# A recurrent two-layer kernel: the experts' gates travel through a DRAM scratch instead of a selection product

## The reference, cut to what matters

```python
xn = layernorm(x)
scores = sigmoid(xn @ gate_w.T)                  # 32 experts
choice = scores + gate_bias                      # 4 groups of 8; best 2 groups, then best 8 experts
w = scores[chosen]; w = w / (w.sum(-1) + 1e-20) * 2.5
g = einsum('th,eih->eti', xn, expert_gate); u = einsum('th,eih->eti', xn, expert_up)
outs = einsum('eti,ehi->eth', silu(g) * u, expert_down)
final = (outs[chosen] * w).sum(1) + shared_mlp(xn)
x = x + attention(xn) * silu(final)
```

## Time and profile before

| what | value |
|---|---|
| median of 3 runs | 594.4 us (592.83 to 595.43) |
| the profiled execution | 595.31 us |
| its span, first to last instruction | 593.6 us |
| outside the span | 1.7 us |
| mean granted clock of PE | 0.953 |
| loop of the first layer's pairs | 44.8 to 243 us of the span |
| scan and second layer | about 250 to 593.6 us |

### The profile page before, as it was taken

How to read it: one execution, slowest core, us unless ns; L and a number is a source line. 1 busy time by engine, 2 the same in 40 slices (tenths; PEclk the granted TensorE clock), 3 DMA queues, 4 the chain that set the end, 5 groups by cost and what they waited for, 6 DMA issues and landing times.

```text
span 593.6 us, 8790 instructions
## 1 busy us (share of the span) xinstructions
PE 532.1 (90%) x2918; PEld 411.9 (69%) x2918; DVE 476.1 (80%) x857; ACT 291.4 (49%) x791; POOL 378.4 (64%) x326
## 2 busy tenths in 40 slices
PE   3978999999999999595899999999999999999865
PEld 3745656666566666384788888888888888888634
DVE  7667775885786586359988999999999999999885
ACT  4431242243225224313666766676667667766523
POOL 6930010012203254443899999999999999999963
PEclk9988999999999999859799999999999999999777
DMA  8440000000000000010011121111111120011002
GB/s 240 154 142 0 2 1 1 1 1 7 12 0 2 18 1 0 15 40 0 19 37 39 33 55 37 31 42 36 54 32 42 36 55 23 31 37 36 19 1 71
DMA packets 16601, 20.81 MB, mean 35 GB/s; under 512 B 2344, under 2 KB 10160, under 8 KB 16428
## 3 DMA queue, kind: packets, MB, share of 16 engines
q1 hardware_dynamic: 16556, 20.26, 11.5%
HBM read 9.76 MB, written 1.05 MB: 18 GB/s over the span
## 4 chain that ended last, share of the span: by engine, by line
POOL 42%; PE 34%; DVE 13%; issue 9%; ACT 1%; DMA 0%; POOLq 0%; DVEq 0%; ACTq 0%
PE bank L560 32%; POOL shared L502 14%; POOL shared L510 7%; POOL shared L488 7%; POOL shared L494 7%; POOL shared L517 6%; PE bank L563 2%; DVE shared L1459 1%; DVE shared L1293 1%; DVE shared L1298 1%; DVE bank L1434 1%; POOL state_ext L524 1%; DVE shared L1216 1%; DVE shared L1208 1%; DVE shared L1428 1%
## 5 line engine op out<-in xcount | busy, mean ns | idle before, releaser
L560 PE MATMUL bank<-xnT_lo,wgu_hi 128*128 128x512 f32 x264 | 121.7, 461 | 11.1 <-ACT shared L1096 7.8
L560 PE MATMUL bank<-w,shared 128*128 128x128 f32 x1024 | 123.6, 279 | 0.3
L560 PEld LDWEIGHTS bank<-w,shared 128*128 128x128 f32 x1024 | 117.7, 193 | 6.2 <-ACT shared L1096 6.2
L560 PE MATMUL bank<-xnT_hi,wgu_lo 128*128 128x512 f32 x264 | 106.0, 402 | 0.0
L560 PE MATMUL bank<-xnT_hi,wgu_hi 128*128 128x512 f32 x264 | 104.9, 397 | 0.0
L502 POOL TENSOR_TENSOR shared<-shared 128x1024 f32<-128x1024 f32 x36 | 86.3, 2399 | 24.6 <-DVE shared L1459 24.6
L560 PE MATMUL bank<-shared 128*128 128x512 f32 (+3 forms) x280 | 90.5, 444 | 2.0 <-ACT shared L944 1.2
L966 ACT ACTIVATE shared<-bank 128x512 f32<-128x512 f32 x68 | 40.6, 597 | 99.0 <-PE bank L560 93.3
L1459 DVE TENSOR_TENSOR shared<-shared,bank 128x2048 f32<-128x2048 f32 x36 | 82.0, 2278 | 5.7 <-PE bank L560 5.7
L1434 DVE TENSOR_REDUCE bank<-shared 128x64 f32<-128x2048 f32 x36 | 82.4, 2288 | 0.3
L1096 ACT ACTIVATE shared<-bank,b 128x512 f32<-128x512 f32 x128 | 81.7, 699 | 0.0
(11 more groups left out here) (175 smaller groups left out, 805.6 us busy)
## 6 DMA issues: line engine op xcount, KB each, us to landing
w<-in_w SPq DMA_DIRECT2D x8, 256.0 KB, 3.1
shared<-in_w SPq DMA_DIRECT2D x1, 2048.0 KB, 9.4
left_tok<-state_ext SPq DMA_DIRECT2D x16, 128.0 KB
left_tok<-state_ext SPq DMA_DIRECT2D x8, 192.0 KB
shared<-in_wd SPq DMA_DIRECT2D x1, 1088.0 KB, 11.8
x<-in_x SPq DMA_DIRECT2D x4, 256.0 KB, 3.5
out<-x SPq DMA_DIRECT2D x4, 256.0 KB, 2.3
left_tok<-state_ext SPq DMA_DIRECT2D x4, 254.0 KB
```

The lines of the kernel that those rows point to most:

```text
L560: return nc.tensor.matmul(out, lhsT, rhs, start=start, stop=stop)
```

## The change

`gate_rows` on PE, its matrix `pair_row`, bank `GB`'s use in the loop, and the split of the gates into three parts are gone. ACT now writes the 32 x 512 gates of a batch in float32 to `gate0T`. SP stores them in a DRAM scratch, waits for the store, and then loads each pair's two rows of 512 gates, each spread over 64 partitions, into a ring of three tiles `gate_rows`. A load for pair n is issued once `h0` of pair n - 3 is made. DVE multiplies by the tile in SBUF and waits for its two DMAs. SP's queue runs in order, so the first two shifts of the scan stand between the loads of later pairs now: `shift(0)` behind those of pair 36, `shift(1)` behind those of pair 52.

```diff
@@ SP
+            def rows_of_gates(n):
+                b, p = divmod(n, PAIRS)
+                if p == 0:
+                    sp.wait_ge(s("g0T_cp"), b + 1)
+                    sp.dma_start(gates_d[b], gate0T[:, b % 2]).then_inc(s("st_gates"), 16)
+                    sp.wait_ge(s("st_gates"), 16 * (b + 1))
+
+                after(sp, s("h0_done"), n - RING + 1)
+                for m in range(2):
+                    sp.dma_start(gate_rows[m * I0:(m + 1) * I0, n % RING],
+                                 gates_d[b, 2 * p + m].partition_broadcast(I0)).then_inc(s(f"ld_rows{n % RING}"), 16)
...
             sp.wait_ge(s("ld_identity"), 16 * B)
+            for n in range(B * PAIRS):
+                rows_of_gates(n)
+                if n == 2 * PAIRS + 4:
+                    shift(0)
+                elif n == 3 * PAIRS + 4:
+                    shift(1)
             for k in range(LEVELS * B):
-                shift(k)
+                if k > 1:
+                    shift(k)
@@ POOL
-            g.tensor_copy(ident_bf[:], ident[:]).then_inc(cdone, 1)
...
-            g.tensor_copy(pair_row[:], pair_sel[:].unsqueeze(2).broadcast_to([3 * E0, E0, I0])).then_inc(sel, 1)
@@ PE
-            def gate_rows(n):
-                b, p = divmod(n, PAIRS)
-                if p == 0:
-                    pe.wait_ge(s("g0T_cp"), b + 1)
-                after(pe, s("h0_done"), n)
-                sel = pair_row[:, 2 * p:2 * p + 2].rearrange("p e i -> p (e i)")
-                mm(bank[GB][:], sel, gate0T[:, b * N:(b + 1) * N]).then_inc(s("gb_mm"), 1)
...
-                    last = tr(bank[MISC if b == 0 else AT][:].bitcast(BF16)[0:3 * E0, j * P:(j + 1) * P],
-                              gate0_parts[:, b * TB + j].rearrange("p a e -> p (a e)"), ident_bf[:])
+                    last = tr(bank[MISC if b == 0 else AT][0:E0, j * P:(j + 1) * P], gates_tok[:, j])
...
-                    gate_rows(n)
@@ ACT
+                after(act, s("st_gates"), 16 * (b - 1))
+                a.copy(gate0T[:, b % 2], bank[MISC if b == 0 else AT][0:E0, :]).then_inc(s("g0T_cp"), 1)
@@ DVE
-                stt(gate0_rest[:], gate0[:], ROUTED, wrec[:].unsqueeze(2).broadcast_to([P, TB, E0]), ALU.mult, ALU.mult).then_inc(step, 1)
-                dve.wait_ge(step, n + 17)
-                v.tensor_copy(gate0_parts[:, tiles, 0], gate0_rest[:]).then_inc(step, 1)
...
-                tt(gate0_parts[:, tiles, 2], gate0_rest2[:], gate0_parts[:, tiles, 1], ALU.subtract).then_inc(s("parts_done"), 1)
+                after(dve, s("g0T_mm"), b)
+                stt(gates_tok[:], gate0[:], ROUTED, wrec[:].unsqueeze(2).broadcast_to([P, TB, E0]), ALU.mult, ALU.mult).then_inc(s("parts_done"), 1)
...
-                dve.wait_ge(s("gb_mm"), n + 1)
+                dve.wait_ge(s(f"ld_rows{n % RING}"), 32 * (n // RING + 1))
...
-                tt(h0[:, n % RING], silu_gu[:, i % 2], bank[GB][:], ALU.mult).then_inc(s("h0_done"), 1)
+                tt(h0[:, n % RING], silu_gu[:, i % 2], gate_rows[:, n % RING], ALU.mult).then_inc(s("h0_done"), 1)
```

More of the change, by code:

```diff
@@ L41 @@
 EXP_LN = "natural_log_exp_and_others"
-SHARED = 23500
+SHARED = 22200
 POLAR = [(8.51425808, -25.281576, 18.7673094), (4.2570752, -3.16016629, 0.586476766),
@@ L120, in build @@
         ident = sb("ident", [P, P])
-        ident_bf = sb("ident_bf", [P, P], BF16)
         ones = sb("ones", [P, P])
@@ L155, in build @@
         head_mask = carve(0, [P, P])
-        pair_sel = sb("pair_sel", [3 * E0, E0], BF16)
-        pair_row = sb("pair_row", [3 * E0, E0, I0], BF16)
         gram = carve(0, [P, B, P + 1])
@@ L192, in build @@
         gate0 = carve(0, [P, TB, E0])
[L193 to L196, removed]
+        gates_tok = carve(0, [P, TB, E0])
+        gate_rows = sb("gate_rows", [P, RING, N])
+        gate0T = sb("gate0T", [E0, 2, N])
+        gates_d = nc.dram_tensor("gate_rows0", (B, E0, N), F32, kind="Internal").ap()
         silu_g = carve(0, [P, 2, N])
@@ L267, in build @@
             "ld_x0 ld_x1 ld_x2 ld_x3 ld_w1 ld_scan ld_gate0 ld_first ld_next ld_attn ld_l1 "
-            "ld_wg ld_wu ld_wd ld_w2_0 ld_w2_1 st_out const sel_done masks "
+            "ld_wg ld_wu ld_wd ld_w2_0 ld_w2_1 st_out const masks "
             "polar_sq_done polar_sum_mm polar_sum_cp polar_r_done polar_x0 ln_stat ln_var_done ln_pow ln_norm "
@@ L271, in build @@
             "woc_done gram_mm gram_cp q_mm q_cp route0_step parts_done g0T_mm g0T_cp "
-            "g_mm u_mm gb_mm silu_done gu_done h0_done dn_mm y0_silu y0T_mm sg_done x1_done "
+            "g_mm u_mm st_gates ld_rows0 ld_rows1 ld_rows2 silu_done gu_done h0_done dn_mm y0_silu y0T_mm sg_done x1_done "
             "m1_mm m1_done st_mm st_done head_mul state_done stT_mm stT_cp so_mm so_cp at_mm at_cp at_stat at_var_done "
@@ L286, in build @@
         LD_ATTN, LD_L1 = 16 * 3, 16 * 5
-        IDENT_READY, CONSTS = 3, 6
+        IDENT_READY, CONSTS = 3, 5
         @block.sync
@@ L769, in _ @@
             gates_to_rows(0)
-            pe.wait_ge(s("sel_done"), 5)
             for b in range(B):
@@ L1035, in gates_out0 @@
                 act.wait_ge(s("g0T_mm"), b + 1)
-                a.copy(gate0T[:, b * N:(b + 1) * N], bank[MISC if b == 0 else AT][:].bitcast(BF16)[0:3 * E0, 0:N]).then_inc(s("g0T_cp"), 1)
+                after(act, s("st_gates"), 16 * (b - 1))
+                a.copy(gate0T[:, b % 2], bank[MISC if b == 0 else AT][0:E0, :]).then_inc(s("g0T_cp"), 1)
             silu_gate(2)
@@ L1200, in shared_hidden @@
                 tt(h_shared[:, b], silu_g[:, b % 2], bank[U[b % 2]][:], ALU.mult).then_inc(s("gu_done"), 1)
-            STEPS = 20
+            STEPS = 16
             def route_groups(b):
```

## The result

The changed kernel takes 595.48 us in the median against 593.14 for the kernel before on the same chip (20 runs each): a ratio of 1.0033, interval 1.0023 to 1.0044. That is "within 0.5%", inside the range of 582 to 597, but 6.5 us above the 589 that I named, and no gain at all. Two of the 20 runs (736 and 623 us, at a granted clock of 0.653 and 0.817) are slow ones, which the interval leaves out; without them the median is 595.37.

The account below looks back on a forecast made before the run. PE was taken to bound the pair loop; -13.7 - 1.9 + 1.5 + 2.3 + 0.3 + 4.8 + 1.5 = -5.2 us took the median from 594.4 to 589, forecast within 586 to 593, overall range 582 to 597.

Parts of the forecast that it names:

- the shifts in the row queue: Pairs 37 and 53: loads issued behind a shift land late, DVE then PE stand; +4.8 us (0 to 8).
- What is removed: Pair loop: 61 gate products of some 0.225 us each come off PE, -13.7 us.
- the earlier waits: Pair loop: PE's waits for DVE (1.1 us) and for the polar chain (0.8 us) go, -1.9 us.
- slots 3 to 5: Batches 1 and 2: faster PE waits at the polar product for `gate_tokens`, 0.75 us each; +1.5 us (0 to 4).
- the batch's turn: Turn of a batch: a store is added before the row load; charged +0.3 us.
- the port: Loop: DVE's two-SBUF-operand products meet POOL, 7 us of DVE, a fifth reaching PE; +1.5 us (0 to 4).
- The start: First pairs: store and load in series delay `h0(0)`, plus 1.5 us for low clock; +2.3 us (0 to 5).
- The loads in the loop: Row loads between slots: some 4 us each for issue and landing, hidden if they land within 6 us.
- What would show it: Signs: loop 7 to 8 us shorter, `h0(0)` near 49.6, DVE waits of 2 to 4 us at pairs 37 and 53.
- half eaten, 594: Rival: half the overruns of DVE's pace, port, shifts and start; 594 us, no change that can be told; chance 0.2.
- The shifts are hidden: Rival: queue not served in order or DVE's slack absorbs the shifts; the 4.8 us drops out, 584 us; chance 0.2.
- Late loads at every pair: Rival: every pair's load is late, three slots lasting product, issue and landing in series; over 600 us; chance 0.07.

Follow-up runs that it names:

- the run with the useless transfers: The late kernel plus two unneeded 127-partition transfers, behind the row loads of pairs 8 and 40; 598.52 us, ratio 1.0078 to the kernel before.
- the shift split: The changed kernel with the 127-partition DMA of the shift split into 112 and 15 partitions; 584.52 us, ratio 0.9836 to the kernel before.
- the control: The kernel before with its 127-partition shift DMA split into 112 and 15 partitions; 594.58 us, ratio 1.0 to the kernel before.
- the run above: The kernel with the shift split, with silu left in PSUM so each DVE product has one operand there; 585.24 us, ratio 0.9849 to the kernel before.
- the late kernel: The changed kernel with the first two shifts whole but behind all row loads in SP's queue; 585.03 us, ratio 0.9838 to the kernel before.

## Why the prediction was wrong

The step that failed is **the shifts in the row queue**, "Together +4.8 us". The mechanism was right, to the pair (37 and 53) and to the engine that waits. The term was mis-sized: it measured 12.2 us (7.8 of idle PE, 4.4 of low clock), and with 12.2 in place of 4.8 my sum would have been +2.2 instead of -5.2, no gain. Of its three parts the first was too low, the second was right, and the third was missing:

- The load's landing. I took 13.3 us behind the shift, from the earlier trace rows, which give 13.7. DVE's product came 15.7 and 15.8 us behind it, and 15.9 and 15.4 in the run with the useless transfers. DVE stood 4.5 and 6.2 us, not 2.8 and 3.8. The trace splits the time: the load that the product needs was issued 5.4 us behind the first shift (the issue ahead of it alone took 3.9), and landed in 10.2 us. In the earlier trace rows that was 4.9 and 8.8. Why the landing took 1.4 us longer than in those rows isn't known: more loads than one stood behind the shift here, but no run separates that. The load's issue, and the landing of all loads from 140 to 160 us (shortest, median, longest):

```profile
146.30 0.60 SPq L326 DMA_DIRECT2D gate_rows<-gate_rows  x1
```

```profile
DMA to landing us min/median/max: 2.7/2.9/10.2
```

- PE's share of it. I left PE 1.4 us of cover at each place. Of DVE's 4.5 us PE stood 3.35, and of 6.2 it stood 4.7. That is a cover of 1.2 and 1.5, so the cover was right and only DVE's time was not. The two 0.5 us for DVE's backlog don't show: PE's idle time grew by 7.8 us, the two stalls are 8.1.
- The clock. I charged a low clock at the start, where the earlier trace rows show one, and none behind the stalls, though I forecast stalls of up to 2.4 us there. It cost 3.4 and 6.8 us at half speed, 5.1 us if all of it had been work, 4.4 by PE's busy time. This was missing from the sum; the idle time alone, 7.8 us, would have stayed under the upper bound of 8.

The rest, in the order of the prediction:

- **What is removed**, the earlier waits, slots 3 to 5, the batch's turn and the port: -13.7 - 1.9 + 1.5 + 0.3 + 1.5 = -12.3 us. With the shift split the loop lost 186.13 - 172.77 = 13.4 us. PE's busy time fell by 181.75 - 167.94 = 13.8. Right within 1.1 us as a sum. PE's idle time rose by 0.45 us (4.38 to 4.83), where my four small terms made +1.4; no run tells them apart. Sixteen slots, from `h0(5)` to `h0(21)`, take 45.1 us where no shift is near, below the 47 that I named.
- **The start**, +2.3: measured 0 at `h0(3)`, give or take a us: in the control, whose start is that of the kernel before, `h0(3)` came 1.2 us earlier (52.84) with 3.4 us of half clock instead of 6.8. `h0(0)` starts at 47.36, not near 49.6, because the store is issued already at 42.17 (the copy ended 2.6 us earlier, not 1.1) and is followed by the first load 1.6 us later, where I took 2.4. The clock is low for 6.8 us there, the same as before in sum. The terms' errors went opposite ways to that of the shifts, else the forecast would have been further off: 7.4 us for the shifts, less 2.3 for the start and 1.1 for the rest, turn -5.2 into -1.2, which is the loop's 1.15. That the time fell inside the range of 582 to 597 is owed in part to this luck.
- **The loads in the loop**: hidden, as said; the run without them is the proof.
- **The port**: 15 products at 0.5 us, 7 us of DVE. Measured 795 - 687 = 108 ns over 64 products, 6.9 us; 14 of them take over 0.72 us, each beside an instruction of POOL. A fifth on the path was 1.5 us; in the run above it was 0.6. The Trainium skill, "SBUF — State Buffer", section "Who interferes with whom", is borne out in kind: single products beside POOL's instructions take up to 1.77 us. (It limits this to GpSimd operations that read SBUF, which the prediction left out.) By its rule alone one would have feared more of this change than it cost.
- **What would show it**: the loop is 1.15 us shorter, not 7 to 8, and PE's waits for DVE in the loop were to stay under 10 us in all. They are 11.2, over the line that I had drawn for "the prediction is wrong":

```profile
PE bank L566 <- DVE shared L1329: 9.9, 6, 4.7
...
PE bank L566 <- DVE shared L1342: 1.3, 2, 1.0
```

**The rivals.** Of "half eaten, 594" the time came true and the mechanism did not: DVE's slack was not used up in many slots, the loss stands at two places. The 594 doesn't follow from its own sum either: half of 21.3 is 10.65, and -15.6 + 10.65 = -4.95 is my forecast again, so that rival had no price of its own. "The shifts are hidden" would have been the split or the late kernel: 584 predicted, 584.5 and 585.0 measured. Late loads at every pair did not happen: the landing is 2.9 us. There, too, a step was wrong: at a landing of 7.6 us three slots would take 8.9 us against 9.4 less three products, 8.7, so a quarter of the gain would be gone and not most of it.

**What stays open.** The profiled spans say -0.7 us, the medians +2.3. Of the difference, 0.4 us lie outside the span (2.1 us after, 1.7 before), 0.4 in the changed kernel's profile, which is below its median, and 2.2 in that of the kernel before, which is above. The 20 runs of the kernel before fall into two groups, ten from 592.4 to 592.83 and ten from 593.45 to 595.43, and both its profiles are from the second. I have no trace of the first group. The granted clock is what tells them apart as far as it was listed: of the 17 runs beside the split kernel, the seven fastest (592.72 to 593.04 us) have 0.961 or 0.962, the other ten (593.18 to 596.06) 0.953 to 0.956. Where in the kernel their clock stays up isn't known. Also, the 12.2 us in the loop are 11.0 in the medians and 10.0 in the spans (592.9 to 582.9): the rest of the span is 355.95 us with the split and 353.81 without. PE is busy for 1.9 us more there (312.97 against 311.06) with the same 2002 products. The stretches of half clock behind the loop add up to some 52 us in either trace, so it isn't their length; they fall on other work, and the 2.1 us arise at two places behind such stretches (near 291 to 296 us and 556 to 562 us of the changed kernel's trace). That the clock is the cause is argued from this, not shown by an experiment.

## What to carry to other kernels

Before a load on which an engine waits joins a queue, look at what else that queue carries. The number to look at is not the bytes but over how many engines the neighbour is spread: a transfer on one engine kept the load behind it in the queue away for nearly 16 us here, and splitting it (127 into 112 and 15) or putting it last costs nothing. And when a stall of PE is priced, look whether the clock falls behind stalls of that length in the trace; here 8.1 us of standing brought 10.2 us at half clock behind it, 4.4 us more by PE's busy time.

## What I had not expected of the hardware

- A DMA issue can hold the issuing engine. Behind a transfer of 127 partitions the next issue took 4.79 us on ACT and 4.17 on SP at the second shift, where such an issue takes 0.65 otherwise. At SP's first shift it was the issue after the next, a row load's, with 3.91; behind ACT's first shift it was none. The kernel before has the same in its queue (3.9 to 4.3 us behind each of its four shifts), where only the load of `w2` stood behind one; behind the two parts of the split shift no issue took over 1.5 us. Behind the four late shifts the issue of the single partition took 4.4, 9.4, 9.8 and 9.8 us on SP. The three long ones stand behind a shift that was issued 5 to 10 us after the last one, in the kernel before that was 11.7 us and more. Whether the earlier shift was still in flight, and is the reason, stays open.
- While a shift is in flight, not all of the traffic stops. The view of the DMA engines for 142.3 to 157.5 us (the GB/s of 40 slices of 0.38 us) shows two bursts of some 200 GB/s, at 147 to 150 and at 152 to 154 us, with 22 to 27 GB/s between them and up to the end of the stall at 156.6. Nothing else but row loads and the shift was issued there. I read it as row loads that run on the other engines while their share on the shift's engine waits:

```profile
GB/s 119 10 23 16 5 22 0 27 27 22 49 27 108 205 210 200 135 210 259 119 22 22 27 22 27 49 205 189 221 81 22 27 27 22 22 27 27 22 27 11
```

- A load of 128 KB lands in 2.9 us in the median, and behind a shift in up to 10.2 us from its own issue. The Trainium skill, "DMA: Bandwidth & Descriptors", section "Queues, rings and completion order", has descriptors of a ring consumed in order; the late landings agree, and so do the row loads that landed in up to 6.3 and 6.9 us, not 10.2, once the shift was on ACT's queue.
